# Weight staging in a recurrent-layer kernel: eight 256-column slots in place of four 512-column slots

## The reference

```python
xn = _layernorm(x)                                   # x: 8 x 4096 x 1024, f32
mixed_q = xn @ Wq + bq
mixed_k = xn @ Wk + bk
q_w = softmax((mixed_q @ Wqa + bqa) * scale, axis=1)          # 16 heads, over the sequence
pooled_q = einsum('bsh,bshd->bhd', q_w, mixed_q)
mixed_qk = mixed_k * pooled_q
k_w = softmax((mixed_qk @ Wka + bka) * scale, axis=1)
pooled_k = einsum('bsh,bshd->bhd', k_w, mixed_qk)
s = (pooled_k * mixed_q) @ Wt + bt + mixed_q
h = square(relu(xn @ W_fc.T)); y = h @ W_proj.T               # 1024 -> 4096 -> 1024
g = silu(mean over 5 steps of the spikes that y drives)       # integrate and fire with reset
out = x + s * g
```

## Time and profile before

| what | us |
|---|---|
| median of the 2 runs | 1802.24 (1798.25 to 1806.22) |
| the profiled execution | 1799.33 |
| its span, slowest core | 1797.2 |
| spans of the 8 cores | 1790.2 to 1797.2 |
| PE busy | 1330.6 (74% of the span) |
| DVE busy | 752.2 (42%) |
| ACT busy | 387.3 (22%) |
| bytes moved by DMA | 174.19 MB, mean 97 GB/s |

### The profile page before, as it was taken

The page is one execution under the profiler, slowest core; times in us unless marked ns, Lnnn a source line. Parts: engine busy times, 40 slices in busy tenths (PEclk is TensorE's granted clock), DMA queues, the critical chain, the costliest instruction groups (busy, mean ns, idle before and its releaser), DMA issues.

```text
span 1797.1 us, 26842 instructions; the slowest of 8 cores (1790.2 to 1797.2 us)
## 1 busy us (share of the span) xinstructions
PE 1330.6 (74%) x8997; PEld 833.0 (46%) x8997; DVE 752.2 (42%) x1337; ACT 387.3 (22%) x836; POOL 155.8 (9%) x284
## 2 busy tenths in 40 slices
PE   0000199999999999999999999999950433519895
PEld 0000066666666666666666666666630121204342
DVE  3211144554553654654644645545340322314443
ACT  1322122132232232221221221321210011011121
POOL 1312100000000000000000000000001011010010
PEclk9999999999999999999999999999975755759998
DMA  5766510110110111111101101101058045147885
GB/s 165 217 187 195 164 60 25 60 54 19 60 48 36 60 42 42 54 41 50 54 30 60 53 30 60 42 19 41 15 175 258 33 162 189 43 144 226 243 246 175
DMA packets 62464, 174.19 MB, mean 97 GB/s; under 512 B 9671, under 2 KB 10071, under 8 KB 62314
## 3 DMA queue, kind: packets, MB, share of 16 engines
q1 hardware_dynamic: 35962, 84.19, 15.6%
q0 software_dynamic: 26368, 88.29, 14.5%
HBM read 121.99 MB, written 50.46 MB: 96 GB/s over the span
## 4 chain that ended last, share of the span: by engine, by line
PE 66%; DMA 18%; DVE 7%; issue 4%; ACT 3%; POOL 0%; SPq 0%; DVEq 0%; ACTq 0%; POOLq 0%
PE PS L483 25%; PE PS L462 24%; PE PS L376 6%; DMA OB<-WprojT 4%; PE PS L852 3%; DMA OB<-WfcT 3%; DMA AM<-cnt_scratch 3%; DMA OB<-WkT 3%; DMA OB<-Wt 2%; PE PS L630 2%; PE PS L380 1%; PE PS L760 1%; ACT YS L492 1%; DVE OB L878 1%; PE PS L344 1%
## 5 line engine op out<-in xcount | busy, mean ns | idle before, releaser
L483 PE MATMUL PS<-AB,AM 128*128 128x512 bf16 x2048 | 533.5, 380 | 15.7 <-ACT YS L492 14.0
L462 PE MATMUL PS<-SCA,AB 128*128 128x256 bf16 x4096 | 530.3, 273 | 0.0
L462 PEld LDWEIGHTS PS<-SCA,AB 128*128 128x128 bf16 x4096 | 400.5, 98 | 153.2
L471 DVE TENSOR_TENSOR AM<-RB 128x256 bf16<-128x256 f32 x512 | 217.2, 424 | 498.4 <-PE PS L483 281.5
L467 ACT ACTIVATE RB<-PS 128x256 f32<-128x256 f32 x512 | 196.7, 384 | 793.2 <-PE PS L462 321.8
L376 PE MATMUL PS<-SCA,AM 128*128 128x256 bf16 x1024 | 138.0, 278 | 187.4 <-DVE SCA L384 167.0
L483 PEld LDWEIGHTS PS<-AB,AM 128*128 128x128 bf16 x2048 | 186.6, 98 | 172.7 <-issue 31.6
L376 PEld LDWEIGHTS PS<-SCA,AM 128*128 128x128 bf16 x1024 | 101.0, 99 | 203.3 <-issue 190.4
L517 DVE SCALAR_TENSOR_TENSOR AM<-YS,AM 128x1024 bf16<-128x1024 f32 x128 | 156.0, 1219 | 0.9
L852 PE MATMUL PS<-AM,AB 128*128 128x512 bf16 x384 | 94.7, 398 | 46.6 <-issue 37.2
L252 DVE CAST AB<-OB 128x512 bf16<-128x512 f32 x80 | 34.1, 427 | 203.4 <-DMA OB<-WfcT 71.1
(11 more groups left out here) (117 smaller groups left out, 778.5 us busy)
## 6 DMA issues: line engine op xcount, KB each, us to landing
XF<-x SPq DMA_DIRECT2D x64, 512.0 KB, 4.7
out<-OB POOLq DMA_DIRECT2D x32, 512.0 KB, 6.7
xn_scratch<-SCA POOLq DMA_DIRECT2D x16, 512.0 KB, 3.1
xtm_scratch<-SCA POOLq DMA_DIRECT2D x32, 256.0 KB, 3.4
mq_scratch<-SCA POOLq DMA_DIRECT2D x16, 512.0 KB, 2.9
cnt_scratch<-AM POOLq DMA_DIRECT2D x32, 256.0 KB, 2.6
AB<-xtm_scratch SPq DMA_DIRECT2D x32, 256.0 KB, 8.8
AM<-cnt_scratch SPq DMA_DIRECT2D x32, 256.0 KB, 5.8
```

The lines of the kernel that those rows point to most:

```text
L462: pl.comp("tensor", lambda te, hb=hb, lt=lt, rh=rh, c=c: te.matmul(hb[:, 0:256], lt, rh, start=(c == 0), stop=(c == 7)), reads=a1keys(c * ...
L471: pl.comp("vector", lambda v, h2=h2, rr=rr: v.tensor_mul(h2, rr, rr), reads=[krr], writes=[("h2", g3)])
L483: pl.comp("tensor", lambda te, yb=yb, lt=lt, rh=rh, j=j: te.matmul(yb[:], lt, rh, start=(j == 0), stop=(j == 31)), reads=[kh2] + a2keys(j ...
```

## The change

In the modes 4 and 2 of `cast_nslots` the pieces are now 256 columns wide (128 KB), and a second table of slots is used. It cuts the same 2048 columns of OB into eight slots, of which the even ones are filled from POOL's queue and the odd ones from SP's. Mode 4 takes all eight and lets eight casts pend; mode 2 takes slots 0, 2, 4 and 6 and lets four pend. Each slot has a semaphore of its own (`ln0` to `ln7`) and a key of its own (`("stgn", i)`). Since the new slots lie on the same bytes as the old ones, each DMA also writes the key of the old slot that it lies in (`okey`): slots 0 and 1 both write `("stgp", 0)`, slots 2 and 3 `("stgp", 2)`, and so on. Mode 8 is as it was. `lmq0` and `lmq1` are cleared and waited for at the end by GpSimd instead of SyncE.

```diff
+        NSEM = {i: f"ln{i}" for i in range(8)}
+        CAST_SLOTS_N = [
+            (("gpsimd", "sync")[i % 2], NSEM[i], OB[:, i * 256:(i + 1) * 256],
+             ("stg", i // 4), ("stgp", (i // 2) * 2))
+            for i in range(8)]
         cast_nslots = [4]
 
         def cast_piece(dsrc_ap, dst_ap, dst_keys):
-            rot = {8: (0, 1, 2, 3, 4, 5, 6, 7), 4: (0, 2, 4, 6),
-                   2: (0, 4)}[cast_nslots[0]]
-            sl = rot[ppc[0] % len(rot)]
-            queue, sem, stg_full, skey = CAST_SLOTS[sl]
+            mode = cast_nslots[0]
+            if mode == 8:
+                sl = ppc[0] % 8
+                queue, sem, stg_full, skey = CAST_SLOTS[sl]
+                wkeys = [(skey[0] + "p", sl)]
+            else:
+                rot = (0, 1, 2, 3, 4, 5, 6, 7) if mode == 4 else (0, 2, 4, 6)
+                sl = rot[ppc[0] % len(rot)]
+                queue, sem, stg_full, skey, okey = CAST_SLOTS_N[sl]
+                wkeys = [("stgn", sl), okey]
             stg = stg_full[:, 0:dsrc_ap.shape[1]]
-            while len(cast_pend) >= min(4, cast_nslots[0]):
+            while len(cast_pend) >= min(4, mode if mode == 8 else
+                                        (8 if mode == 4 else 4)):
                 cast_pend.pop(0)()
             pl.dma(queue, sem, lambda g, a=dsrc_ap, s=stg: g.dma_start(s, a),
-                   reads=[], writes=[(skey[0] + "p", sl)])
+                   reads=[], writes=wkeys)
@@
-            cast_pend.append(lambda s=stg, d=dst_ap, k=list(dst_keys), sl=sl,
-                             en=ceng, m=meth, sk=skey: pl.comp(
+            cast_pend.append(lambda s=stg, d=dst_ap, k=list(dst_keys),
+                             rk=wkeys[0], en=ceng, m=meth, sk=skey: pl.comp(
                 en, lambda eng, s=s, d=d, m=m: m(eng, s, d),
-                reads=[(sk[0] + "p", sl)], writes=k + [sk]))
+                reads=[rk], writes=k + [sk]))
@@
             w = dsrc_ap.shape[1]
-            if w > 512:
-                for o in range(0, w, 512):
-                    cast_piece(dsrc_ap[:, o:o + 512], dst_ap[:, o:o + 512], dst_keys)
+            pw = 512 if cast_nslots[0] == 8 else 256
+            if w > pw:
+                for o in range(0, w, pw):
+                    cast_piece(dsrc_ap[:, o:o + pw], dst_ap[:, o:o + pw], dst_keys)
```

More of the change, by code:

```diff
@@ L29 @@
              "lw0", "lw1", "lw2", "lw3", "lw4", "lw5", "lw6", "lw7",
+             "ln0", "ln1", "ln2", "ln3", "ln4", "ln5", "ln6", "ln7",
              "l30", "l31", "l32",
@@ L179, in build_nc @@
         GP_SEMS = ("pool", "lw0", "lw1", "lw4", "lw6", "sx0", "sx1",
-                   "tm0", "tm1", "mq0", "mq1", "sq", "sc0", "sc1", "so0", "so1")
+                   "ln0", "ln2", "ln4", "ln6",
+                   "tm0", "tm1", "mq0", "mq1", "sq", "sc0", "sc1", "so0", "so1",
+                   "lmq0", "lmq1")
         SY_SEMS = ("lc", "lw2", "lw3", "lw5", "lw7", "l30", "l31", "l32",
-                   "lb0", "lb1", "ltm0", "ltm1", "lmq0", "lmq1", "lqs",
+                   "lb0", "lb1", "ltm0", "ltm1", "lqs",
+                   "ln1", "ln3", "ln5", "ln7",
                    "cr0", "cr1")
@@ L215, in build_nc @@
             pl.res[k]["w"] = lc_tot
-        BIAS_FINE = {"bq": [("stgp", 0), ("stgp", 2)], "bk": [("stgp", 4), ("stgp", 6)],
+        BIAS_FINE = {"bq": [("stgp", 0), ("stgp", 2)] + [("stgn", i) for i in range(4)],
+                     "bk": [("stgp", 4), ("stgp", 6)] + [("stgn", i) for i in range(4, 8)],
                      "bt": [("ysp", 1), ("ysp", 3)], "bqa": [("ysp", 5)],
```

## The result

The changed kernel takes 1824.13 us in the median of 11 runs (1820.52 to 1838.51), the kernel before 1798.68 us in the median of 10. The ratio is 1.0144, with a 95% interval of 1.012 to 1.0168: slower, by less than the 2% that the prediction's chances count as a change.

A forecast was written before the change was run, and what follows sets the result against it. The prediction took the startup to be bound by a ring of waits, with no engine full. Startup +30, later loads +4, +8, +7 and -2 sum to +47 on the profiled 1799.3 us: 1846 us, range 1808 to 1888.

The forecast's parts named there:

- the 0.34: Whole kernel: chance given to a time within 2% (36 us) of before, which counts as no change.
- L in part 4: Startup loads: landing time of one 128 KB piece, taken as 3.1 us, between 2.3 and 4.5.
- The ring of waits: Startup: paired slots wait for each other's landing, so a round is two landings plus 0.67 us, 6.87 against 5.61.
- No hold-up on the queues: POOL's and SP's queues: waiting DMAs hold back only their own queue's other slots, at no further cost.
- The casts: DVE and ACT casts at 256 columns: 0.30 and 0.40 us, 3.5 us per round, hidden beside the transfers.
- 66 L - 157: Whole kernel: summed change in us by landing time; zero at 2.4 us, +36 at 2.9, +80 at 3.6.
- The DMA engines: Startup: 3.7 to 5.1 us of engine time per round, under 6.87, so not the bound.
- rival C: SP's 1 KB rows cost as much per packet as 2 KB rows; landing above 3.6 us, over 1880 us; chance 0.15.
- Startup: Weight loading before the main loop: 24 rounds, each longer by 6.87 - 5.61 us, +30 us.
- The later loads: Weight loads after startup: Wt +4, Wk +8, last Wt +7, WkT -2 us.
- Rival B: Startup and later loads: half-size pieces land in 2.3 us, 1794 us, not slower; chance 0.16.
- Rival D: Startup and later loads: pairing does not bite, round 4.5 us, 1763 us, faster by 2%; chance 0.04.

The follow-up runs named there:

- run with alternating roles: Kernel before, with eight 256 KB slots for all startup weights, neighbours paired by a shared key, firsts and seconds alternating between POOL's and SP's queues: 1896.55 us, ratio 1.0548.
- run with large pairs and the roles kept apart: Kernel before, with eight paired 256 KB slots for all startup weights, every pair's first on POOL's queue and second on SP's: 1785.49 us, ratio 0.993.

## Why the prediction was right, and where its size was off

The direction and the mechanism were right, and the time lay in the range; the size was nearly twice too large (+47 for +25), and "slower by over 2%", to which I gave 0.62, did not come about. The case that did was the 0.34. What failed is the size of one term, L in part 4.

- **The ring of waits** (part 2) is what the trace shows: POOL released by SP's landing, SP by POOL's, in every step of the chain above. The handoffs were 0.54 and 0.07 us in the steps shown, 0.61 together for 0.67. Undoing the pairing alone turns the loss into a gain.
- **No hold-up on the queues** (part 2, "this costs nothing more"): nearly right for this change. At times POOL is still issuing for another pair: a landing at 116.62 was answered at 118.17, 1.55 us later instead of 0.54, as these pieces of the chain show. And it is more fragile than the sentence sounds: the run with alternating roles shows 111 us for it.

```profile
113.10 3.52 DMA OB<-WprojT
...
117.17 0.44 POOL OB L265
...
118.17 2.93 DMA OB<-WprojT
```

- **The casts** (part 3): 0.29 and 0.41 us for 0.30 and 0.40, beside the transfers as said. The ACT casts wait for DMA in 77 cases of 90 and DVE for ACT; none of it is in the chain from 108 to 136 us.
- **The landing L** (part 4) is the term that was mis-sized. I took 3.1 us; it was 3.0 on the slowest core of the profiled execution, 2.9 on its neighbour and 2.6 to 2.7 on the other six, 2.7 in the mean. The sum's formula, 66 L - 157, gives +22 us for 2.71 and +41 for 3.0. That the first is near the measured +24 is in part luck: the stages that it adds up lost 28 us, and the closing DRAIN, which it does not have, gave 4.5 back. The step that failed is the one from 4.5 us to 3.15: 1.8 fixed, and 2.7 for the bytes halved to 1.35. The runs with 128 KB pieces give 2.7 us with 0.5 MB in flight and 3.8 with 1 MB, a line of 1.6 fixed and 1.1 for each half megabyte; those with 256 KB give 3.1 and 4.5, 1.7 and 1.4. So the fixed part was 0.1 to 0.2 us too large, and for the small pieces the part that goes with the bytes too, 1.35 for 1.1. Whether small pieces pay less than large ones for the same bytes in flight isn't settled by this: in the run with large pairs and the roles kept apart, pieces of 256 KB with up to 1 MB in flight land in 4.1 us and not in 4.5, so something beside size and bytes, such as when the pieces go out, counts too. That the small pieces without pairs land in the same 2.7 us says that the pairing is not what shortened it. Of the rows that I had, the 3.0 us for 256 KB with little beside it was nearer than the 4.5.
- **The DMA engines** (part 5): 57.8% of 125 us for 19.56 MB is 3.9 us for a round, inside 3.7 to 5.1 and near the lower end, so the engines weren't the bound. An SP packet takes 0.294 x 16 x 125 / 10672 = 0.055 us, against 0.081 before; POOL's transfers are 48 packets each. The window has 2388 packets under 512 B for 150 transfers, 16 each, which I take for the completions; so the 128 rows of 1 KB went in 32 packets, four rows each, where two rows of 2 KB went in one before. The sign that I had named for rival C did appear: SP's share rose from 26.0% to 29.4% at a lower rate. It was a poor sign, since it shows only that a packet of half the bytes costs more than half: SP's part of a round rose from 1.5 to 2.0 us, not to the 2.9 of rival C, and L stayed below its 3.6. Rival C is out.
- **Startup**: +15 in the mean for +30, and an L 0.4 lower is worth 24 x 2 x 0.4 = 19 us, more than the 15 that are missing. The rounds were thus longer than the formula has them, by the mean about 6.2 us where 2 x 2.71 + 0.61 is 6.0; POOL's late issues, as above, are one part of it. On core 1, with L = 3.0, PE starts 25.5 us later.
- **The later loads**: +2.3, +6.9, +5.9 and -2.3 us for +4, +8, +7 and -2. Their order is right, which fits the two reasons given for Wk and the last Wt, that less is loaded ahead; no run tests these by themselves.
- **The end of the program** (put at nothing): -4.5 us, the closing DRAIN.
- **Rival B** (two short landings, no change) had the right sign of my error: the landing came 0.4 us below my value, but not the 0.7 it needed. The rule of the Trainium skill that spoke for it ("DMA: Bandwidth & Descriptors", section "Anatomy of one DMA"), a fit to transfers that GpSimd issues, gives an estimate of 2.3 us for 128 KB. The trace does not agree with it in this stage: 2.6 to 3.0 with up to four in flight, 3.8 with up to eight.
- **Rival D** (eight slots run freely, 1763 us) did not happen here, and with the pairing undone it gave 1780: its round was 4.9 us and not 4.5, with landings of 3.8 us at twice the bytes in flight, and from the first pooling to the output loop it gained 1 us in the mean of the cores where I had put 9.

## What to carry to other kernels

A loader that waits for slots is a ring: its rate is the bytes in flight divided by one turn (landing, use, reissue), so before more or smaller slots are added, count the bytes that can be in flight at once. A key or buffer that two slots share turns them into one slot with two landings; here that took away more than the whole gain of eight slots over four. If such sharing can't be avoided, let all firsts go out on one queue and all seconds on another, or the waits will hold up the next pair as well. And add up the stages to the very end of the span: here 4.5 us lay in the last instruction of a queue, behind all the work, and without them one experiment looks like a miss.

## What the runs showed of the hardware that I had not expected

With up to 1 MB in flight, pieces of 128 KB land in 3.8 us and pieces of 256 KB in 4.5 us, so twice as many small pieces give 216 GB/s where the large give 187. It isn't the size alone: large pieces in pairs, with up to 1 MB in flight too, land in 4.1 us and give 232. With up to 0.5 MB in flight it is 2.7 to 3.0 against 3.1 us: there twice the piece costs 0.1 to 0.4 us. All eight cores loading together reached 295 GB/s on the slowest core with 2 MB in flight, at a DMA share of 0.95, where the kernel before had stopped at 187. And within one execution the landing of the same transfers differed by core, 2.9 and 3.0 us on cores 0 and 1 against 2.6 to 2.7 on the others, at the same clock; over 24 rounds this spread the start of the main loop by 22 us (from 235.8 to 258.2), where before it was 6 (226.3 to 232.6). In the two profiled executions with the new staging in the startup alone it is cores 0 and 1 again (the main loop starts at 255 to 256 us there, and at 239 to 247 on the others), but in other executions of the changed kernel the longest spans are those of cores 2 and 3, or hardly any core stands out. Why, no run here tells. The DRAIN that ends POOL's queue took 4.06, 8.06 or 8.55 us, depending on the kernel, the same on all eight cores, and it lies wholly behind the last store.
